# Order and size of the first weight loads of a two-layer fused kernel: two more tiles of the second weights ahead of what is left of the first weights' row tiles

## What is computed

```python
def cond(x, W0, b0, A, B, s, ids):           # L0; L1 has no scale
    return x @ W0.T + b0 + s[ids] * ((x @ A[ids].T) @ B[ids].T)
def ffn(y, W1, b1, Wr, loraA, loraB):        # top-2 of 8 experts, scaling 2
    w = renormalized_top2(softmax(y @ Wr.T))
    return y @ W1.T + b1 + 2 * sum_e w_e * ((y @ loraA_e.T) @ loraB_e)
x = x + ffn0(cond0(x));  x = x + ffn1(cond1(x))
```

## Time and profile before

| what | value |
|---|---|
| median of 3 runs | 687.23 us (686.88 to 687.95) |
| the profiled execution | 687.59 us |
| span in its trace | 685.8 us |
| PE busy | 680.0 us, 99% |
| DVE busy | 421.5 us, 61% |
| ACT busy | 233.5 us, 34% |
| POOL busy | 261.3 us, 38% |
| moved by DMA | 147.24 MB, mean 215 GB/s |

### The profile page before, as it was taken

One profiled execution on the slowest core, in us unless ns is written; L12 is line 12 of the kernel. 1 busy time (PEld: TensorE's weight loads), 2 busy tenths in 40 slices (PEclk: granted clock), 3 DMA queues, 4 the chain that ended last, 5 costly groups with the idle time before them and its releaser, 6 DMA issues.

```text
span 685.8 us, 9221 instructions
## 1 busy us (share of the span) xinstructions
PE 680.0 (99%) x3309; PEld 600.7 (88%) x3309; DVE 421.5 (61%) x705; ACT 233.5 (34%) x429; POOL 261.3 (38%) x217
## 2 busy tenths in 40 slices
PE   8999999999999999999999999999999999999997
PEld 7999999888888888888899999998888888888886
DVE  5664668768855473862663753886698437738423
ACT  6444245644131034220514344266252302422200
POOL 2373023027593150395133432030647625105920
PEclk9999999999999999999999999999999999999999
DMA  8355756992868934547742755689836886535633
GB/s 298 109 159 180 261 198 209 390 380 108 263 186 321 343 117 130 157 141 258 281 170 72 231 169 183 246 275 375 332 122 216 291 333 195 175 117 171 192 113 122
DMA packets 74131, 147.24 MB, mean 215 GB/s; under 512 B 6948, under 2 KB 38308, under 8 KB 73958
## 3 DMA queue, kind: packets, MB, share of 16 engines
q1 hardware_dynamic: 70678, 138.20, 59.0%
q10 hardware_dynamic: 1872, 6.36, 3.0%
q0 software_dynamic: 1536, 2.10, 1.1%
HBM read 98.42 MB, written 47.33 MB: 213 GB/s over the span
## 4 chain that ended last, share of the span: by engine, by line
PE 97%; DMA 1%; SPq 1%; ACT 0%; DVE 0%; issue 0%
PE ps L599 45%; PE ps L481 15%; PE ps L482 15%; PE ps L483 15%; PE ps L558 4%; PE ps L615 2%; DMA e_raw<-in_ext 1%; PE ps L608 1%; SPq L281 0%; PE ps L498 0%; PE ps L581 0%; ACT e_hl L710 0%; SPq L258 0%; DVE w_hl L972 0%; DVE w L1177 0%; ACT w_hl L719 0%
## 5 line engine op out<-in xcount | busy, mean ns | idle before, releaser
L599 PE MATMUL ps<-x_hl,a_hl 128*128 128x512 f32 x1344 | 317.7, 394 | 0.0
L599 PEld LDWEIGHTS ps<-x_hl,a_hl 128*128 128x128 f32 x1344 | 251.1, 188 | 53.6 <-issue 0.3
L481 PE MATMUL ps<-e_hl,w_hl 128*128 128x384 f32 (+1 forms) x432 | 145.8, 338 | 0.6 <-DVE e_hl L972 0.5
L482 PE MATMUL ps<-e_hl,w_hl 128*128 128x384 f32 (+1 forms) x432 | 145.8, 338 | 0.0
L483 PE MATMUL ps<-e_hl,w_hl 128*128 128x384 f32 (+1 forms) x432 | 145.6, 337 | 0.0
L481 PEld LDWEIGHTS ps<-e_hl,w_hl 128*128 128x128 f32 x432 | 81.5, 189 | 1.8 <-issue 1.0
L482 PEld LDWEIGHTS ps<-e_hl,w_hl 128*128 128x128 f32 x432 | 81.4, 188 | 0.0
L483 PEld LDWEIGHTS ps<-e_hl,w_hl 128*128 128x128 f32 x432 | 81.4, 188 | 0.0
L972 DVE TENSOR_TENSOR x_hl<-x_raw,x_hl 128x512 fp32r<-128x512 f32 x64 | 60.8, 1004 | 8.9 <-ACT x_hl L806 8.9
L1353 POOL TENSOR_TENSOR w<-x_raw 128x512 f32<-128x512 f32 x16 | 23.8, 1515 | 104.6 <-DMA x_raw<-in_xT 34.0
L972 DVE TENSOR_TENSOR w_hl<-w_raw,w_hl 128x1024 fp32r<-128x1024 f32 (+2 forms) x24 | 20.6, 869 | 57.2 <-ACT w_hl L697 50.3
(11 more groups left out here) (115 smaller groups left out, 900.1 us busy)
## 6 DMA issues: line engine op xcount, KB each, us to landing
a_hl<-form_scratch SPq DMA_DIRECT2D x112, 512.0 KB, 5.2
form_scratch<-f_hl SPq DMA_DIRECT2D x56, 512.0 KB, 7.4
e_raw<-in_ext SPq DMA_DIRECT2D x12, 580.0 KB, 8.6
w_raw<-in_w ACTq DMA_DIRECT2D x12, 512.0 KB, 3.3
x_raw<-in_xT SPq DMA_DIRECT2D x6, 1024.0 KB, 8.0
x_raw<-x_scratch SPq DMA_DIRECT2D x6, 1024.0 KB, 7.0
x_scratch<-x_raw SPq DMA_DIRECT2D x16, 256.0 KB, 3.1
out_T<-x_raw SPq DMA_DIRECT2D x16, 256.0 KB, 3.3
```

Of the source, the lines that this page charges most:

```text
L481: nc.tensor.matmul(dst, w_hi, m_hi, start=start, stop=False, skip_group_check=again)
L482: nc.tensor.matmul(dst, w_hi, m_lo, start=False, stop=False, skip_group_check=again)
L599: last = nc.tensor.matmul(ps[:, bank, :], a_hl[:, n % NM, k, w, :], x_hl[:, slot, k, x, :], start=start and i == 0, stop=i == 3 * KH - 1, ...
```

## The change

E4 is loaded ahead of the rest of r0, and E5 ahead of the rest of r1; ACT and DVE take them in that order too, both in pieces (`PIECED = 4` tiles are split piece by piece, before three). So that PE can use E4 before the rest of r0 is there, block 4 comes with block 1: the second load of each row tile is two blocks (128 KB, strided) where it was one. The rest then has five blocks and comes in two transfers, blocks 5 to 7 (192 KB) and blocks 2 and 3 (128 KB), with a cast and a subtraction for each part. E1 is loaded in one transfer of 580 KB, where it was three; it is still split in three pieces. PE's wait for the rest of a row tile moves from its step with E4 to its step with E5.

```diff
@@ SP, load_first @@
-                pieces(0)
+                for ob, (o, n) in enumerate(OB):
+                    sp.dma_start(e_raw[:, 0, 1, o:o + n], ext[l, 0:P, o:o + n]).then_inc(d_ep[ob], 16)
...
                 w0_start(sp, l, 0, 1)
                 w0_start(sp, l, 1, 1)
-                pieces(1)
-                sp.dma_start(w0_raw[:, 0, 1, 2 * P:D], w0[l, k_of(0), :, 2 * P:D]).then_inc(d_w0[0], 16)
+                load_e(l, 1)
...
                 load_e(l, 4)
-                sp.dma_start(w0_raw[:, 1, 1, 2 * P:D], w0[l, k_of(1), :, 2 * P:D]).then_inc(d_w0[1], 16)
+
+                def load_w0_rest(r):
+                    for cols, done in zip(W0_RESTS, (d_w0[r], S[("d_w0j", "d_w1j")[r]])):
+                        sp.dma_start(w0_raw[:, r, 1, cols], w0[l, k_of(r), :, cols]).then_inc(done, 16)
+
+                load_w0_rest(0)
                 load_e(l, 5)
+                load_w0_rest(1)
                 load_e(l, 6)
@@ PE, fold @@
-                    elif i == 2:
+                    elif i == PIECED - 1:
                         pe.wait_ge(S["w0_lo"], RT * l + r + 1)
-                    elif r == 0:
-                        pe.wait_ge(S["e_lo"], (KT - 3) * l + i - 2)
+                    elif i >= PIECED and r == 0:
+                        pe.wait_ge(S["e_lo"], (KT - PIECED) * l + i - PIECED + 1)
@@ ACT and DVE, first @@
                 for ob in range(NOB):
                     piece(1, ob)
+                for ob in range(NOB):
+                    piece(2, ob)
                 rest_of(0)
                 for ob in range(NOB):
-                    piece(2, ob)
+                    piece(3, ob)
                 rest_of(1)
```

More of the change, by code:

```diff
@@ L73 @@
 E_ORDER = (0, 1, 4, 5, 6, 2, 3, 7)
+PIECED = 4
 def k_of(r):
@@ L112, in fused_layers @@
         d_w0 = [S["d_w0a"], S["d_w0b"]]
-        d_e = {k: ctx.enter_context(nc.semaphore(f"d_e{k}")) for k in E_ORDER[2:]}
-        d_ep = [ctx.enter_context(nc.semaphore(f"d_ep{i}")) for i in range(2 * NOB)]
+        d_e = {k: ctx.enter_context(nc.semaphore(f"d_e{k}")) for k in E_ORDER[1:]}
+        d_ep = [ctx.enter_context(nc.semaphore(f"d_ep{i}")) for i in range(NOB)]
         d_xk = [ctx.enter_context(nc.semaphore(f"d_xk{i}")) for i in range(KT)]
@@ L253, in by_tile, with blocks_of @@
             return v.rearrange("p (k b r) -> p k b r", k=KT, b=BATCH)
+        def blocks_of(buf, r, hl, i):
+            tile = buf[:, r, hl, :].rearrange("p (k n) -> p k n", k=KT)
+            return tile[:, 0:1, :] if i == 0 else tile[:, 1:5:3, :]
         def w0_start(eng, l, r, i):
-            cols = slice(i * P, (i + 1) * P)
-            eng.dma_start(w0_raw[:, r, 1, cols], w0[l, k_of(r), :, cols]
+            src = w0[l, k_of(r)].rearrange("p (k n) -> p k n", k=KT)
+            eng.dma_start(blocks_of(w0_raw, r, 1, i), src[:, 0:1, :] if i == 0 else src[:, 1:5:3, :]
                           ).then_inc(S[(("d_w0h", "d_w1h"), ("d_w0i", "d_w1i"))[i][r]], 16)
+        W0_RESTS = slice(5 * P, D), slice(2 * P, 4 * P)
         block = ctx.enter_context(nc.Block())
@@ L512, in fold @@
                         pe.wait_ge(S["w0h_lo"], 4 * l + 2 + r + 1)
-                    elif i == 2:
+                    elif i == PIECED - 1:
                         pe.wait_ge(S["w0_lo"], RT * l + r + 1)
-                    elif r == 0:
-                        pe.wait_ge(S["e_lo"], (KT - 3) * l + i - 2)
+                    elif i >= PIECED and r == 0:
+                        pe.wait_ge(S["e_lo"], (KT - PIECED) * l + i - PIECED + 1)
                     for ob in range(NOB):
-                        if i < 3 and r == 0:
-                            pe.wait_ge(S["ep_lo"], 3 * NOB * l + i * NOB + ob + 1)
+                        if i < PIECED and r == 0:
+                            pe.wait_ge(S["ep_lo"], PIECED * NOB * l + i * NOB + ob + 1)
                         last = fold_unit(r, k, ob, i == 0, i == KT - 1)
@@ L705, in piece @@
                     k, (o, n) = E_ORDER[i], OB[ob]
-                    if i < 2:
-                        act.wait_ge(d_ep[i * NOB + ob], 16 * (l + 1))
+                    if i == 0:
+                        act.wait_ge(d_ep[ob], 16 * (l + 1))
                     else:
@@ L712, in start @@
                 def start(r, i):
-                    cols = slice(i * P, (i + 1) * P)
                     act.wait_ge(S[(("d_w0h", "d_w1h"), ("d_w0i", "d_w1i"))[i][r]], 16 * (l + 1))
-                    nc.scalar.copy(w0_hl[:, r, 0, cols], w0_raw[:, r, 1, cols]).then_inc(S["w0h_hi"], 1)
+                    nc.scalar.copy(blocks_of(w0_hl, r, 0, i), blocks_of(w0_raw, r, 1, i)).then_inc(S["w0h_hi"], 1)
                 def rest_of(r):
+                    last, first_part = W0_RESTS
                     act.wait_ge(d_w0[r], 16 * KH * l + 16)
-                    nc.scalar.copy(w0_hl[:, r, 0, 2 * P:D], w0_raw[:, r, 1, 2 * P:D]).then_inc(S["w0_hi"], 1)
+                    nc.scalar.copy(w0_hl[:, r, 0, last], w0_raw[:, r, 1, last])
+                    act.wait_ge(S[("d_w0j", "d_w1j")[r]], 16 * (l + 1))
+                    nc.scalar.copy(w0_hl[:, r, 0, first_part], w0_raw[:, r, 1, first_part]).then_inc(S["w0_hi"], 1)
                 if l:
@@ L733, in first @@
                     piece(1, ob)
+                for ob in range(NOB):
+                    piece(2, ob)
                 rest_of(0)
                 for ob in range(NOB):
-                    piece(2, ob)
+                    piece(3, ob)
                 rest_of(1)
             def rest(l):
-                for k in E_ORDER[3:]:
+                for k in E_ORDER[PIECED:]:
                     e_split(l, k)
@@ L994, in start @@
                 def start(r, i):
-                    cols = slice(i * P, (i + 1) * P)
                     dve.wait_ge(S["w0h_hi"], 4 * l + 2 * i + r + 1)
-                    sub(w0_hl[:, r, 1, cols], w0_raw[:, r, 1, cols],
-                        w0_hl[:, r, 0, cols].bitcast(f32)).then_inc(S["w0h_lo"], 1)
+                    sub(blocks_of(w0_hl, r, 1, i), blocks_of(w0_raw, r, 1, i),
+                        blocks_of(w0_hl, r, 0, i).bitcast(f32)).then_inc(S["w0h_lo"], 1)
                 def rest_of(r):
+                    last, first_part = W0_RESTS
                     dve.wait_ge(S["w0_hi"], RT * l + r + 1)
-                    sub(w0_hl[:, r, 1, 2 * P:D], w0_raw[:, r, 1, 2 * P:D],
-                        w0_hl[:, r, 0, 2 * P:D].bitcast(f32)).then_inc(S["w0_lo"], 1)
+                    sub(w0_hl[:, r, 1, last], w0_raw[:, r, 1, last], w0_hl[:, r, 0, last].bitcast(f32))
+                    sub(w0_hl[:, r, 1, first_part], w0_raw[:, r, 1, first_part],
+                        w0_hl[:, r, 0, first_part].bitcast(f32)).then_inc(S["w0_lo"], 1)
                 if l:
@@ L1017, in first @@
                     piece(1, ob)
+                for ob in range(NOB):
+                    piece(2, ob)
                 rest_of(0)
                 for ob in range(NOB):
-                    piece(2, ob)
+                    piece(3, ob)
                 rest_of(1)
             def rest(l):
-                for i in range(3, KT):
+                for i in range(PIECED, KT):
                     e_split(l, i)
@@ L1214, in _ @@
                 dve.wait_ge(S["d_bias"], 32 * (l + 1))
-                dve.wait_ge(S["e_lo"], (KT - 3) * (l + 1))
-                dve.wait_ge(S["ep_lo"], 3 * NOB * (l + 1))
+                dve.wait_ge(S["e_lo"], (KT - PIECED) * (l + 1))
+                dve.wait_ge(S["ep_lo"], PIECED * NOB * (l + 1))
                 for r in range(KT):
```

8 lines of the change are left out of this document (4 added, 4 removed).

## The result

Slower by a quarter of a per cent: 689.23 us (median of 22 runs, 687.83 to 691.11) against 687.70 (22 runs, 686.88 to 687.98), a ratio of 1.0024 with an interval of 1.0018 to 1.0030. The prediction was 686.5 us, -0.1%; the time came out 1.5 us above the kernel before and outside the range. Two things stand in this result. The middle has moved up, and the spread is three times as wide: 3.3 us, where it was 1.1. The runs fall into two groups. In 12 the mean granted clock is 0.999 or 1.0, and their median is 688.58; in 10 it is 0.997 or 0.998, and their median is 689.96.

What follows compares the result with a forecast made beforehand. PE was taken to bound the kernel, busy 680.0 of 685.8 us, so only its idle time could be won. Terms -1.32 + 0.5 + 0.1 = -0.7 us gave a median of 686.5 us (-0.1%), range 685.7 to 687.8.

Steps and rivals of the forecast that it cites:

- What bounds the kernel: Whole kernel: PE is busy 680.0 of 685.8 us, so only time in which PE stands still can be won.
- the three holes: Layer 0, PE's holes before r0 with E4, r1 with E4 and r0 with E5: all go, -1.32 us.
- The new wait for E1: Layer 0, before r0 with E1: E1 lands whole at 8.8, PE starts at 10.05, +0.5 us (0 to +1.1).
- the late end: Layer 0, upper bound for E1's landing: bytes land as before, so 1544 KB are there at 9.40.
- rival (d): Layer 0, wait at 9.64: PE's clock falls for some 4 us, costing 1.8 us; sum +1.1, 688.3 us; chance 0.03.
- Its premise on the first matmuls: Layer 0: matmuls every 0.32 us at first are PE's 1.2 GHz, every 0.175 us from 8.06 on its 2.4 GHz.
- The layer border: Before layer 1's fold: E5's subtractions move ahead of results on DVE, which may come late: +0.1 us (0 to +0.9).
- rival (c): Layer border: DVE reaches `out_c21` after 340.75, costing 0.9 us with E5 at 338.35; sum +0.6, 687.8 us; chance 0.11.
- "Nothing else changes": Elsewhere: same first loads, bytes and matmuls; row tiles 2 to 7 keep their distance to PE; no term.
- Rival (a): Layer 0: E1's large transfer lands by 8.39 or nearly so, border has room: -1.1 to -1.3 us, 686.0; chance 0.17.

Runs made afterwards that it cites:

- E4: Not a run or kernel: a data tile of 580 KB, whose load the change puts ahead of the rest of r0.
- E5: Not a run or kernel: a data tile of 580 KB, whose load the change puts ahead of the rest of r1.
- the kernel with pieces and the new border: Changed kernel with E1 in three pieces and, at the layer border, DVE's subtractions for E5 and the rest of r1 behind the eight results: 686.66 us, ratio 0.9986.
- the held kernel: Changed kernel with E4's load, and all behind it, held back in layer 0 until E1 has landed: 688.77 us, one execution.
- the stretch with the granted clock at 0.50 above: From the trace of the changed kernel with E4 issued ahead of E1 in layer 0: 691.41 us, one execution.
- the kernel with pieces: Changed kernel with E1 loaded in three pieces again, each used as it lands, and a rest's two transfers counted on one semaphore: 687.40 us, ratio 1.0002.
- the one with a hole of 1.36 us: Kernel before the change with only E1's load made one transfer of 580 KB: 687.26 us, ratio 0.9998.
- the first experiments: Those with E1 in pieces, one part of the change alone, or eight more matmuls before layer 0's r0 with E1; kernel before beside them: median 687.50 us.

## Why the prediction was wrong

*What bounds the kernel, and the three holes (-1.32 us).* Right. In every trace of the changed kernel the steps with E4 and E5 follow without a hole, and the kernel with pieces and the new border shows that most of this can be had: 1.0 us.

*The new wait for E1 (+0.5 us, 0 to +1.1).* Right in kind and wrong in size, and this is the step that failed. PE's hole measured 2.40, 2.29, 1.53 and 2.07 us. E1 landed at 9.9 to 10.5 where the late end said 9.40. That end took the bytes of what had landed for all that had been moved, as if the engines took one transfer after the other. They don't: in the changed kernel some 2400 KB had been moved when E1's 1544 were complete. In the held kernel E1 landed at 9.1; E4 and what follows it cost 0.8 to 1.4 us. The trace of before held the warning. Its stretches up to the landing of E1's last piece at 8.74, and from there to that of the rest of r0 at 10.73, read:

```profile
0.00:8.74 8.74, 7.14 (x22) 6.20 (x23) 3.63 (x10) 4.61 (x10) 3.58 (x8) 1.00 0.68 200
8.74:10.73 1.99, 1.99 (x14) 1.99 (x13) 1.17 (x3) 0.56 (x2) 0.00 (x0) 1.00 0.93 355
```

That is about 1710 KB moved at 8.74, where I counted 1416, and 690 KB more by 10.73, where I counted 384. The engines moved 355 GB/s there, not far below the steady 410; what looked slow was mostly work on the transfers behind.

The size of the term is read from when the step starts. It started at 11.48, 11.77, 11.13 and 11.52, against 9.64 before and a forecast of 10.05. With the 0.1 behind the hole the term is +1.6 to +2.2, in the middle +1.9, where +0.5 stood. (The holes are up to 0.6 us longer than this, because PE was due at the step sooner than 9.64, which wins nothing.) With -1.3 it makes +0.6, and r1 with E5 indeed starts 0.2 to 0.9 us later than before: at 19.45, 19.77, 19.10 and 19.52, against 18.86. The 12 runs at full clock are 688.58 - 687.70 = 0.9 above. Of the 0.3 between, the hole before row tile 2 explains 0.3 in the first trace, 0.15 in the second and nothing in the other two; the rest stays open.

*The clock, rival (d), 0.03.* Much too low. The argument against it was that 0.6 us did not make the clock fall, which says nothing of a hole four times as long; the two questions hung together, and the chance should have been tied to the size of the hole. Its premise on the first matmuls was not read from the profile either: they run every 0.32 us, as in the stretch with the granted clock at 0.50 above, but the granted clock reads 1.00 there. In 10 of 22 runs the time is 1.4 us longer at a lower mean clock (689.96 against 688.58), which I put down to the fall; no trace of the changed kernel shows it. With both groups the median is 1.5 above.

*The layer border (+0.1, 0 to +0.9).* Right for the changed kernel: no hole in four traces, `out_c21` starting 4.55, 4.68, 4.23 and 4.63 us ahead of the fold where 4.24 were needed. Its mechanism and the deadline of 4.24 us before the fold came true elsewhere: in the kernel with pieces `out_c21` started 2.74 us before the fold's due time of 344.64, and PE's fold was 1.40 us late (0.16 more stood before one of layer 0's last products), where 4.24 - 2.74 gives 1.50. So rival (c) was real. It stayed away in the changed kernel because E4 landed sooner there: at most 6.6 us behind ACT's first cast of a layer-1 block, against 8.2 in the kernel with pieces (7.1 in the one with both). Whether the one transfer of E1 brings that about is not shown.

*"Nothing else changes".* Nearly. The load of row tile 2 took 4.0, 3.8, 3.5 and 3.3 us where it took 3.3 in the trace of before, and its slack of 0.4 us was not enough in the first trace (a hole of 0.22 us) and the second (0.04). It is not the change alone: with the old order and E1 whole it took 3.9 us and left the same 0.22. What makes it long is not shown. I had called that distance fixed without asking how much slack there was in it.

*Rival (a)*, the large transfer that is fast, failed clearly. By the fit of the Trainium skill, "DMA: Bandwidth & Descriptors", section "Anatomy of one DMA", 580 KB would take 3.4 us (an estimate from its figures); measured were 6.5, and 5.4 with E4 held back. The page gives the fit for one DMA on the path of GpSimd, and these loads are started by SP and have others in flight beside them. The prediction left that out and used the fit where the page doesn't claim it.

## What to carry to other kernels

Where an engine waits for the first of several loads, what counts is not only what is queued ahead of it. Here the large transfers issued right behind it delayed its last bytes by 0.8 to 1.4 us. So let a load that is needed at once come in pieces or have nothing large behind it. Before counting bytes by landings, compare them with what the engines have moved by then; here the difference was work on later transfers. A load moved forward also moves its preparation forward in in-order streams; ask which results stand behind it, and work out their deadline. And a long hole of PE can have a second price, the clock. Look for it in the spread and the mean clock of the runs, since one profile may not catch it.

## What the runs showed of the hardware

- Two transfers of 580 KB issued 0.5 us apart took 6.5 and 7.4 us to land, 1.4 us apart; the first alone, with the second held, took 5.4. The DMA engines were 0.97 to 1.01 busy in 7 to 10 us in the first case, at 325 to 361 GB/s. When the first had landed, some 850 KB of what was asked for behind it had been moved (560 to 1090 KB in the four traces).
- After a hole of 3.66 us TensorE's clock stayed at its upper level for four matmuls (0.8 us), then lay at half for some 3.5 us. After holes of 0.6 to 2.4 us no trace shows a fall; in the timed runs of the kernel with holes of 1.5 to 2.4 us 10 of 22 have a mean clock of 0.997 or 0.998, of the one with a hole of 1.36 us 1 of 11, and none of the 33 runs of the kernel before that stand beside the first experiments has (0.999 or 1.0).
- PE's first matmuls of the fold run every 0.32 us and then every 0.175, and where that changes is not fixed: at 7.5 us in the trace of before and at 6.4 in the first one of the changed kernel, with the same work ahead of it, so that r1 with E0 began at 8.06 and at 7.51. The granted clock reads 1.00 on both sides of the change, so the profile does not show this slow start as a lower clock. The difference was swallowed by the next wait for data in both.
